# A start list and a written order for the filling and emptying of a software-pipelined two-layer graph transformer (fp32, one core)

## The chip, the cores and the metric

One core of a Trainium2 chip. The metric is the device time of one execution in microseconds; the median of three runs is shown. The engines are PE (matmul), ACT, DVE, POOL and SP, which here only issues DMAs. Each engine works through its own instruction list in order, and they meet by semaphores.

## The reference

For a batch of 128 graphs with 128 nodes and 256 channels, two layers follow one another.

```
layer A: q,k,v = x@W.T + b; 8 heads of 32; p = softmax(where(adj, q k^T, -16384))
         z = v; four times z = 0.9 * p @ z + 0.1 * v
         x = layernorm(x + z) * gamma + beta
layer B: n = ln1(x); q,k,v = n@w + b
         p = softmax(q k^T / sqrt(32) + (0.1*adj*adj where adj > 0, else -inf))
         x1 = x + (p @ v) @ wo + bo
         out = x1 + gelu(ln2(x1) @ w1 + b1) @ w2 + b2      # 256 -> 1024 -> 256
```

All is float32. The kernel keeps precision in large matmuls by splitting each operand into a rounded high part (fp32r) and a low part, the rest, and adds three products: high by high, high by low, low by high.

## The kernel before

Graphs are taken in pairs (`GB = 2`), 64 pairs `g`. The work of a pair is cut into 84 named steps, each a small function on each engine that takes part. Names: `lt`, `lx`, `laA`, `laB` load x turned (`xT`), x and the adjacency (SP); `xs` splits `xT` into `inT_A` (POOL, L657); `qA kA vA` project (PE L309 and L318, copied out by ACT and, for `vA`, DVE); `msA` masks (POOL); `sA` scores of all heads (PE L327); `mA00` to `mA11` add the mask and take maxima (DVE L534; digits: graph, half of the heads); `eA..` exps (ACT L437); `rA0`, `rA1` reciprocals (DVE); `wA0`, `wA1` normalise (POOL L678); `pA..` transpose the probabilities (PE L341, out by ACT for half 0, by DVE for half 1); `z0` to `z3` the hops (PE L357, out by ACT), each with `h0` to `h3`, which turns the result back (PE L367, out by DVE); `xv` prepares the residual (POOL). Layer norms are `y` (statistics, DVE), `i` (root, POOL), `n` (normalise, DVE), numbered 0 to 2; `g`, `b1`, `b2` add rows (POOL). `tB`, `tC` transpose a normalised input (PE L293; high part by ACT, low part by DVE). Layer B repeats `q k v s m e r w p` and then has `pv` (PE L376), `o` (L383), `u0` to `u3` (up, PE L391, gelu on ACT L463), `c0` to `c3` (low parts, DVE L612), `d0`, `d1` (down, PE L401), `st` (store).

What sets the order is one list, `ORDER`, with a lag beside each step: in turn i every engine goes through the list and does step `n` for pair `i - lag`. Lags go from 0 (`kA`, `qA`) to 5 (`tC`, `u`, `c`, `d`, `st`), so there are 64 + 5 = 69 turns, 0 to 68; in turns 0 to 4 and 64 to 68 steps whose pair does not exist are left out. `Timetable` (L85) builds the list. It also deals out the four PSUM banks of `ring_ps` in list order. Most buffers are single; `v_A`, `xv` and `probsT_A` are double.

Before the list there is a set-up (L229 to L233 on SP, L262 on PE, L478 on DVE). All 24 parameter tensors are loaded into space that the pairs use later (`probs`, `probsT_A`, `probsT_B`) with one semaphore, and PE, ACT, DVE and POOL wait for the whole of it:

```
WEIGHTS = 16 * (9 + 9 + 6)
pe.wait_ge(s_weights, WEIGHTS)      # so do ACT, DVE and POOL
```

PE then does the fold (52 small matmuls, L268 and L271: the shifts of the layer norms times the weights, to go into the biases), DVE adds it to the biases, scales the weights of layer B by the layer norms' gains, and writes all high parts, then all low parts. `s_ready` releases PE and ACT. POOL and SP begin the steps before that.

Of the kernel before, what the change touches and what calls it, by code (L numbers as in the profile page):

```python
# [96 lines left out]

def build(nc, x, xT, adj, WqT, bq, WkT, bk, WvT, bv, gamma, beta, ln1_g, ln1_b, ln2_g, ln2_b,
# [648 lines left out]
```

## Time and profile before

| | us |
|---|---|
| median of 3 runs | 2346.55 (2343.37 to 2348.0) |
| the profiled execution | 2345.26 |
| its span, first to last instruction | 2343.5 |
| granted TensorE clock, mean of the span | 0.995 |

The span is what the trace shows; 1.8 us of the profiled execution's own time lie around it. Times in rows are in microseconds from the span's start. Consecutive matmuls overlap, so a piece of PE work is best read from the start of one to the start of the next.

### The profile page before, as it was taken

Reading aid. Unit: us, or ns where it says so; the run is one execution under the profiler, and the core shown is the slowest. Engines: PE = TensorE matmul, PEld = TensorE weight load, DVE = VectorE, ACT = ScalarE, POOL = GpSimd, SP = SyncE. Lnnn points to the kernel's source line nnn. Section 1 sums busy time; section 2 is a strip of 40 time slices with the busy share of each in tenths; the row PEclk is TensorE's granted clock in tenths of the full one; section 3 lists DMA queues with packets and bytes.
Section 4 is the critical chain, followed back from the end, with each engine's and each line's share of the span. In section 5 each row is a group of like instructions: output and inputs, shape, how many; then the busy total and the mean of one; then the engine's idle time right before and its main releaser. Section 6 shows DMA issues by size and latency. Waiting matters only on the chain.

```text
span 2343.5 us, 77819 instructions
## 1 busy us (share of the span) xinstructions
PE 2262.8 (97%) x29492; PEld 2154.7 (92%) x29492; DVE 1729.5 (74%) x7009; ACT 1915.3 (82%) x6462; POOL 1515.4 (65%) x1610
## 2 busy tenths in 40 slices
PE   2799999999999999999999999999999999999987
PEld 2689999999999999999999999999999999999987
DVE  3478778778777777777777777877877877877863
ACT  0679889889889888888888888888988988988964
POOL 0676766666667666666666676676676666666652
PEclk9999999999999999999999999999999999999999
DMA  3110110110110110110111011011011011011000
GB/s 96 36 33 20 38 38 21 37 38 24 34 38 24 34 38 25 33 38 27 31 38 36 22 38 38 20 38 38 20 38 38 20 38 38 25 34 38 20 15 15
DMA packets 95729, 76.85 MB, mean 33 GB/s; under 512 B 9600, under 2 KB 95104, under 8 KB 95360
## 3 DMA queue, kind: packets, MB, share of 16 engines
q1 hardware_dynamic: 95360, 71.87, 10.0%
q8 instruction: 239, 3.92, 0.7%
q14 instruction: 130, 1.06, 0.1%
HBM read 55.06 MB, written 16.78 MB: 31 GB/s over the span
## 4 chain that ended last, share of the span: by engine, by line
PE 93%; ACT 3%; DVE 1%; issue 1%; POOL 0%; DMA 0%; ACTq 0%; DVEq 0%; POOLq 0%
PE ring_ps L290 41%; PE ring_ps L407 15%; PE ring_ps L353 13%; PE ring_ps L345 10%; PE score_ps L336 6%; PE ring_ps L373 5%; PE ring_ps L300 3%; ACT probs L441 1%; ACT hidden L469 0%; ACT hT_high L469 0%; POOL probs L683 0%; DVE w_low L506 0%; ACT zT L455 0%; DVE probs L541 0%; ACT L469 0%
## 5 line engine op out<-in xcount | busy, mean ns | idle before, releaser
L441 ACT ACTIVATE probs<-probs,negmax 128x128 f32<-128x128 f32 x2048 | 796.5, 397 | 11.7 <-DVE negmax L541 4.6
L683 POOL TENSOR_TENSOR probs<-probs,rinv 128x512 f32<-128x512 f32 x512 | 533.4, 1063 | 102.1 <-DVE rinv L555 101.9
L441 ACT ACTIVATION_READ_ACCUMULATOR probs<-probs,negmax 128x1 f32 x2048 | 399.8, 195 | 0.0
L455 ACT ACTIVATE zT<-ring_ps 128x512 f32<-128x512 f32 x256 | 158.4, 619 | 211.4 <-PE ring_ps L353 211.4
L290 PE MATMUL ring_ps<-inT_C_high,w_high 128*128 128x256 f32 x1024 | 301.7, 295 | 1.4 <-DVE inT_C_low L522 1.4
L345 PE MATMUL ring_ps<-ident,probs 128*128 128x128 f32 x2048 | 294.0, 276 | 6.6 <-POOL probs L683 4.8
L407 PE MATMUL ring_ps<-w_high,hT_high 128*128 128x256 f32 x1024 | 296.8, 290 | 2.0 <-ACT hT_high L469 1.5
L407 PE MATMUL ring_ps<-w_low,hT_high 128*128 128x256 f32 x1024 | 286.5, 280 | 0.0
L407 PE MATMUL ring_ps<-w_high,hT_low 128*128 128x256 f32 x1024 | 286.2, 279 | 0.0
L290 PE MATMUL ring_ps<-inT_C_high,w_low 128*128 128x256 f32 x1024 | 285.0, 278 | 0.0
L290 PE MATMUL ring_ps<-inT_C_low,w_high 128*128 128x256 f32 x1024 | 285.0, 278 | 0.0
L614 DVE TENSOR_TENSOR hT_low<-hidden,hT_high 128x512 fp32r<-128x512 f32 x256 | 223.2, 872 | 71.7 <-ACT hT_high L469 64.5
L345 PEld LDWEIGHTS ring_ps<-ident,probs 128*128 128x128 f32 x2048 | 227.7, 141 | 33.2 <-issue 27.2
L541 DVE CUSTOM_DVE_ANT_0 probs<-score_ps,mask_B 128x128 f32<-128x128 f32 x1024 | 228.5, 283 | 32.6 <-PE score_ps L336 32.6
L689 POOL TENSOR_TENSOR rstd<-moments,eps 128x2 f32<-128x2 f32 x192 | 37.8, 197 | 311.2 <-DVE moments L601 311.0
L541 DVE CUSTOM_DVE_ANT_0 probs<-score_ps,mask_A 128x128 f32<-128x128 f32 x1024 | 229.3, 283 | 7.8 <-issue 7.3
L469 ACT ACTIVATE hidden<-ring_ps,b_col 128x256 f32<-128x256 f32 x512 | 219.9, 494 | 5.0 <-PE ring_ps L290 4.2
L587 DVE TENSOR_TENSOR x<-ring_ps,x1b 128x512 f32<-128x512 f32 x64 | 44.3, 691 | 241.0 <-PE ring_ps L290 239.1
L469 ACT ACTIVATE hT_high<-ring_ps,b_col 128x256 fp32r<-128x256 f32 x512 | 222.0, 506 | 0.0
L353 PE MATMUL ring_ps<-probsT_A,z 128*32 128x128 f32 x6144 | 207.6, 276 | 7.5 <-DVE z L568 7.4
L290 PEld LDWEIGHTS ring_ps<-inT_C_high,w_high 128*128 128x128 f32 x1024 | 194.1, 190 | 2.4 <-DVE inT_C_low L522 2.0
L407 PEld LDWEIGHTS ring_ps<-w_high,hT_high 128*128 128x128 f32 x1024 | 192.4, 188 | 2.9 <-ACT hT_high L469 2.0
(148 smaller groups left out, 7362.7 us busy)
## 6 DMA issues: line engine op xcount, KB each, us to landing
xT_sb<-in_xT_dram SPq DMA_DIRECT2D x64, 256.0 KB, 3.2
x_sb<-in_x_dram SPq DMA_DIRECT2D x64, 256.0 KB, 2.9
out_dram<-x SPq DMA_DIRECT2D x128, 128.0 KB, 2.0
adj_A<-in_adj_dram SPq DMA_DIRECT2D x64, 128.0 KB, 3.1
adj_B<-in_adj_dram SPq DMA_DIRECT2D x64, 128.0 KB, 2.3
probsT_A<-in_L_gnn_w_dram SPq DMA_DIRECT2D x1, 1024.0 KB, 7.7
probsT_B<-in_L_gnn_w_dram SPq DMA_DIRECT2D x1, 1024.0 KB, 10.1
probs<-in_L_gnn_Wq_dram SPq DMA_DIRECT2D x1, 256.0 KB, 2.9
```

The lines of the kernel that those rows point to most:

```text
L290: mm = pe.matmul(dst, left(a, kc), right(b, kc), start=(n == 0), stop=(n == len(pairs) - 1))
L336: mm = pe.matmul(score_ps[:, r, (b * C + c) * P:(b * C + c + 1) * P], qT[l][r * HD:(r + 1) * HD, c, b * P:(b + 1) * P], kT[l][r * HD:(r + ...
L345: mm = pe.transpose(ring(name, g)[:, r * P:(r + 1) * P], probs[:, UNIT[l, b], half * HR + r, :], ident[:, :])
L353: mm = pe.matmul(ring(name, g)[r * HD:(r + 1) * HD, (b * C + c) * P:(b * C + c + 1) * P], src[:, b, h * HD:(h + 1) * HD], prT[:, b, h, :], ...
L373: mm = pe.transpose(ring(name, g)[:, at:at + P], zT[k][:, b, c, :], ident[:, :])
L407: mm = pe.matmul(ring(name, g)[:, 0:H], hT[a][:, f, b * P:(b + 1) * P], w2_p[c][:, f, :], start=(n == 0), stop=(n == len(pairs) - 1))
L441: e = act.activation(probs[:, u, h, :], probs[:, u, h, :], ACT.Exp, bias=negmax[:, u, h:h + 1], scale=-1.0, accum_out=sums[:, u, h:h + 1])
L455: act.activation(zT[k][:, :, :, :], ring(name, g).rearrange("p (b c n) -> p b c n", b=GB, c=C), ACT.Copy).then_inc(s_out[name], 1)
L469: e = act.activation(dst[:, i, :], ring(name, g)[:, i * T:(i + 1) * T], ACT.Gelu, bias=b1_col[:, 2 * f + i:2 * f + i + 1])
L541: t = dve.tensor_tensor_reduce(probs[:, u, h, :], score_ps[:, r, (b * C + half) * P:(b * C + half + 1) * P], mask[l][:, b, :], -1.0, HIGHE ...
L614: dve.tensor_tensor(hT[1][:, 2 * f:2 * f + 2, :], hidden[:, f % 2, :, :], hT[0][:, 2 * f:2 * f + 2, :], ALU.subtract).then_inc(s_h_low[nam ...
L683: pool.tensor_tensor(probs[:, u, hs, :], probs[:, u, hs, :], rinv[:, u, hs].unsqueeze(2).to_broadcast([P, HR, P]), ALU.mult).then_inc(s_pr ...
```

## The change

Three things, and what they need.

1. The start. Loads are issued in order of use, with ten semaphores instead of one; five small ones go out from ACT's queue. The first `xT`, adjacency and x are part of SP's start list. The three layer-A weights are split right away, each by its own ACT copy and DVE subtraction. All other set-up work becomes steps of the list, done once, in pair 0: `Wf` (the fold), `Wq Wk Wv`, `Wo`, `Wu0 Wu1`, `Wd0` to `Wd3` (high part on ACT with the gain as its scale; low part on DVE, for `Wd` on POOL). Raw weights lie in layer-B buffers only.
2. The first nine turns (0 to 8) and the last eight (61 to 68) are replaced by lists of their own, `HEAD` and `TAIL`, which hold the same steps of the same pairs in another order. In `TAIL` the number is the distance from the end: `.1` is the last pair.
3. Because the order differs there, steps in those lists and in turns 9 to 11 (`table.loose`) wait explicitly for the readers of the buffer that they overwrite; some semaphores are shared between steps and waited for by their count in the list (`table.nth`).

The PE steps in the two lists, in the order of the change:

```
HEAD: qA.0 kA.0 vA.0 sA.0 qA.1 kA.1 vA.1 sA.1 pA00.0 pA01.0 qA.2 pA10.0 pA11.0 kA.2 z0.0 h0.0 sA.2 z1.0 pA00.1 pA01.1 h1.0
 pA10.1 z2.0 pA11.1 h2.0 z0.1 z3.0 h0.1 h3.0 z1.1 vA.2 h1.1 Wf.0 z2.1 qA.3 h2.1 tB.0 z3.1 pA10.2 pA11.2 h3.1 kB.0 ...
TAIL: ... sB.4 z1.3 pv.5 d1.6 ... qB.3 kB.3 pA00.1 sB.3 tC.4 pA10.1 pA11.1 vA.1 pA01.1 vB.3 u0.4 z0.1 u1.4 pB00.3 pB01.3 u2.4
 h0.1 tB.2 u3.4 pB10.3 pB11.3 kB.2 qB.2 pv.3 z1.1 sB.2 d0.4 d1.4 h1.1 o.3 z2.1 h2.1 pB00.2 z3.1 pB01.2 h3.1 tC.3 vB.2
 pB10.2 u0.3 u1.3 pB11.2 u2.3 u3.3 pv.2 d0.3 tB.1 d1.3 qB.1 kB.1 o.2 sB.1 vB.1 tC.2 u0.2 u1.2 u2.2 u3.2 pB10.1 pB00.1
 pB11.1 pB01.1 d0.2 pv.1 d1.2 o.1 tC.1 u0.1 u1.1 u2.1 u3.1 d0.1 d1.1
```

The core of the diff:

```diff
+HEAD_TURNS = 9
+HEAD = """
+eb.0 qA.0 lx.0 laB.0 xs.0 laA.0 kA.0 eA00.0 vA.0 mA00.0 sA.0 msA.0 eA01.0 xs.1 mA01.0 lt.0 qA.1 lt.1 mA10.0 mA11.0
+kA.1 rA0.0 vA.1 mA00.1 sA.1 eA10.0 eA11.0 pA00.0 eA00.1 rA1.0 lt.2 pA01.0 qA.2 mA01.1 pA10.0 xv.0 msA.1 pA11.0 eA01.1
+wA0.0 rA0.1 xs.2 wA1.0 msB.0 Wd2.0 kA.2 z0.0 mA10.1 eA10.1 wA0.1 eA11.1 mA11.1 h0.0 sA.2 msA.2 wA1.1 z1.0 pA00.1 rA1.1
+Wd0.0 pA01.1 xv.1 h1.0 Wq.0 mA00.2 pA10.1 Wd3.0 z2.0 pA11.1 h2.0 Wv.0 Wu1.0 z0.1 z3.0 Wd1.0 i0.0 h0.1 xs.3 h3.0 y0.0
+g.0 Wk.0 z1.1 eA00.2 mA01.2 n0.0 mA10.2 vA.2 h1.1 eA01.2 msA.3 Wu0.0 mA11.2 y1.0 eA10.2 Wo.0 i1.0 Wf.0 eA11.2 rA1.2
...
+TAIL_TURNS = 8
...
-        self.steps = [(n, i - lag) for i in range(pairs + DEPTH) for n, lag in ENTRIES if 0 <= i - lag < pairs]
+        turns = [[(n, i - lag) for n, lag in ENTRIES if 0 <= i - lag < pairs] for i in range(pairs + DEPTH)]
+        head = [(n, int(g)) for n, g in (t.split(".") for t in HEAD.split())]
+        tail = [(n, pairs - int(g)) for n, g in (t.split(".") for t in TAIL.split())]
+        turns[:HEAD_TURNS] = [head]
+        turns[len(turns) - TAIL_TURNS:] = [tail]
+        self.steps = [s for turn in turns for s in turn]
+        self.loose = set(head + tail + [s for turn in turns[1:4] for s in turn])
...
         @block.sync
-            for t, w in loads: ...  for t, w in cols: ...  for t, w in rows: ...
+            weight(rawA["q"][:, :, :], WqT, "Aq")
+            sp.dma_start(xT_sb[:, :, :], xT_v[0]).then_inc(s_xT, 16)
+            weight(rawA["k"][:, :, :], WkT, "Ak")
+            weight(rawA["v"][:, :, :], WvT, "Av")
+            sp.dma_start(adj_sb["A"][:, :, :], adj_v[0]).then_inc(s_adj["A"], 16)
+            for n, w in (("q", wq), ("k", wk), ("v", wv)):
+                weight(rawB[n], w, "B")
+            weight(w1_raw, w1, "up")
+            column(h2_col, ln2_b, "up")
+            column(g2_col, ln2_g, "up")
+            sp.dma_start(x_sb[:, :, :], x_v[0]).then_inc(s_x, 16)
+            weight(rawB["o"], wo, "o")
+            for f, t in enumerate(w2_raw):
+                sp.dma_start(t[:, :, :], w2.rearrange("(c p) n -> p c n", p=P)[:, 2 * f:2 * f + 2, :]).then_inc(s_in["down"], 16)
+            for t, w in ((colB["q"], lbq), (colB["k"], lbk), (b1_col, b1)):
+                column(t, w, "rest")
+            for t, w in ((bvB_row, lbv), (gamma_row, gamma), (beta_row, beta), (bo_row, bo), (b2_row, b2)):
+                row(t, w, "rest")
...
         @block.tensor
-            pe.wait_ge(s_weights, WEIGHTS)
...
             def input_ready(g, l, n):
                 if l == "A":
                     pe.wait_ge(s_split, g + 1)
+                    if g == 0:
+                        pe.wait_ge(s_wA, "qkv".index(n) + 1)
...
         @block.scalar
+            for t, w, signal in ((colA["q"], bq, "colA"), (colA["k"], bk, "colA"), (h1_col, ln1_b, "B"), (g1_col, ln1_g, "B")):
+                act.dma_start(t[:, :], w.rearrange("(c p) -> p c", p=P), allow_slow_non_contiguous=True).then_inc(s_in[signal], 16)
+            act.dma_start(bvA_row[:, :], bv.partition_broadcast(P)).then_inc(s_in["bvA"], 16)
+            for n in "qkv":
+                act.wait_ge(s_in["A" + n], 16)
+                act.activation(wA[n][0][:, :, :], rawA[n][:, :, :], ACT.Copy).then_inc(s_whighA, 1)
+            def split_w(name, g, n):
+                act.wait_ge(s_in["B"], 16 * 5)
+                for kc in range(C):
+                    w = act.activation(wB[n][0][:, kc, :], rawB[n][:, kc, :], ACT.Copy, scale=g1_col[:, kc:kc + 1])
+                w.then_inc(s_whigh, 1)
...
         @block.vector
+            for done, n in enumerate("qkv"):
+                dve.wait_ge(s_whighA, done + 1)
+                dve.tensor_tensor(wA[n][1][:, :, :], rawA[n][:, :, :], wA[n][0][:, :, :], ALU.subtract).then_inc(s_wA, 1)
...
             def values(name, g, l):
-                if l == "A" and g:
-                    dve.wait_ge(s_xv, g)
+                if l == "A" and g >= 2:
+                    dve.wait_ge(s_xv, g - 1)
+                    dve.wait_ge(s_out["h2"], g - 1)
```

## Rows read from the trace of the kernel before

**Rows 1.** The page: busy time by engine, share of the span, instructions.
```profile
PE 2262.8 (97%) x29492; PEld 2154.7 (92%) x29492; DVE 1729.5 (74%) x7009; ACT 1915.3 (82%) x6462; POOL 1515.4 (65%) x1610
```

**Rows 2.** Chain of waits, whole span: start, length, what; the turn repeats.
```profile
203.95 2.83 PE ring_ps L290 x24
...
238.82 2.83 PE ring_ps L290 x24
...
2192.10 2.83 PE ring_ps L290 x24
```

**Rows 3.** Timeline of the start: start, length, engine, line, what [idle before].
```profile
0.72 0.44 SPq L229 DMA_DIRECT2D probs<-in_L_gnn_Wq_dram  x1
...
5.30 3.46 SPq L231 DMA_DIRECT2D colA_q<-in_L_gnn_bq_dram  x1
...
19.15 8.05 SPq L238 DMA_DIRECT2D xT_sb<-in_xT_dram  x2
24.07 0.48 DVE L482 TENSOR_SCALAR h_wide<-ones,h_col 128x128 f32<-128x128 f32 x2 [24.07 <-DMA b_row<-in_L_gnn_b_dram]
...
34.93 2.05 PE L271 MATMUL ring_ps<-probs,h_wide 128*128 128x256 f32 x4
...
54.28 0.58 PE L290 MATMUL ring_ps<-inT_A_high,wA_k_high 128*128 128x256 f32 x1 [17.30 <-DVE w_low L506]
```

**Rows 4.** DMA issues of 0 to 30 us: queue, size, median us to landing.
```profile
xT_sb<-in_xT_dram SPq DMA_DIRECT2D x2, 256.0 KB, 4.2
probs<-in_L_gnn_Wq_dram SPq DMA_DIRECT2D x1, 256.0 KB, 2.9
...
b_row<-in_L_gnn_b_dram SPq DMA_DIRECT2D x1, 128.0 KB, 5.4
```

**Rows 5.** Timeline again: first pieces of POOL, DVE and ACT, and matmuls.
```profile
24.84 0.61 POOL L662 CAST inT_A_high<-xT_sb 128x512 fp32r<-128x512 f32 x1 [23.14 <-DMA xT_sb<-in_xT_dram]
25.53 1.27 POOL L664 TENSOR_TENSOR inT_A_low<-xT_sb,inT_A_high 128x512 fp32r<-128x512 f32 x1
...
45.52 0.69 DVE L506 TENSOR_TENSOR wA_q_low<-probs,wA_q_high 128x512 fp32r<-128x512 f32 x1
...
57.32 1.28 ACT L433 ACT_TABLE_LOAD   x1 [57.32 <-PE ring_ps L290]
...
58.68 0.28 PE L290 MATMUL ring_ps<-inT_A_high,wA_q_low 128*128 128x256 f32 x1
```

**Rows 6.** Chain of waits, 54 to 146 us: start, length, what.
```profile
62.54 3.19 ACT probs L441 x16
...
74.03 1.05 PE ring_ps L353 x32
...
92.47 0.70 DVE y L574
...
101.94 0.88 PE ring_ps L300 x4
...
145.24 0.44 PE ring_ps L300 x4
```

**Rows 7.** Chain of waits, 2200 us to the end.
```profile
2203.16 0.44 PE ring_ps L300 x4
...
2231.66 1.10 PE score_ps L336 x32
...
2263.97 1.10 PE score_ps L336 x32
...
2294.23 1.15 PE score_ps L336 x32
...
2314.44 1.01 PE ring_ps L353 x32
```

**Rows 8.** Busy time by stretch (instructions), granted clock last but two.
```profile
1017.08:1051.96 34.88, 34.88 (x463) 33.32 (x461) 26.76 (x110) 29.95 (x103) 23.69 (x26) 1.00 0.10 33
...
54.28:101.94 47.66, 35.21 (x484) 30.63 (x485) 21.65 (x111) 27.51 (x104) 24.01 (x25) 0.96 0.09 26
```

More of the change, by code:

```diff
@@ new lines @@
+eA01.7 tB.5 eA10.7 pB11.4 mA11.7 eb.5 rA1.7 eA11.7 d1.3 h1.6 i0.5 qB.5 rA0.7 lt.8 kB.5 pv.4 mB00.5 z2.6 sB.5 pA00.7
+mB01.5 o.4 eB00.5 y2.4 wB1.4 pA10.7 h2.6 qA.8 g.5 mB10.5 kA.8 eB01.5 i1.5 n2.4 pA11.7 st.3 pA01.7 mB11.5 z3.6 msB.5
+laB.6 rB0.5
+"""
+TAIL_TURNS = 8
+TAIL = """
+laA.4 lt.3 h3.6 xs.4 wA0.5 tC.8 y0.6 eB10.7 z0.5 wA1.5 vA.4 eB11.7 eb.6 vB.7 h0.5 u0.8 sA.4 mA00.4 n0.6 z1.5 pB00.7
+xv.5 c0.8 u1.8 i2.8 lx.5 h1.5 msA.4 u2.8 u3.8 rB1.7 qA.3 z2.5 c1.8 c2.8 b1.7 mA01.4 pB10.7 xs.3 c3.8 y1.6 pB01.7
@@ L73 @@
     KINDS[f"d{_b}"] = ("down", _b)
+SET_UP = {"Wf": ("fold",), "Wo": ("split_o",)}
+for _n in "qkv":
+    SET_UP[f"W{_n}"] = ("split_w", _n)
+for _k in range(C):
+    SET_UP[f"Wu{_k}"] = ("split_up", _k)
+for _k in range(FC // 2):
+    SET_UP[f"Wd{_k}"] = ("split_down", _k)
 ENTRIES = [(t.split("/")[0], int(t.split("/")[1])) for t in ORDER.split()]
@@ L79 @@
 assert sorted(NAMES) == sorted(KINDS)
-RINGED = ("turn", "project", "values", "turn_probs", "hop", "turn_back", "attend", "output", "up", "down")
+KINDS.update(SET_UP)
+RINGED = ("fold", "turn", "project", "values", "turn_probs", "hop", "turn_back", "attend", "output", "up", "down")
+PER_LAYER = ("maxima", "exps", "recip")
+SHARED = {k: (k,) for k in PER_LAYER + ("low",)}
+SHARED.update({k: ("split",) for k in ("split_w", "split_o", "split_up", "split_down")})
 UNIT = {(l, b): 2 * "AB".index(l) + b for l in "AB" for b in range(GB)}
@@ L88, in __init__ @@
     def __init__(self, pairs):
-        self.steps = [(n, i - lag) for i in range(pairs + DEPTH) for n, lag in ENTRIES if 0 <= i - lag < pairs]
+        turns = [[(n, i - lag) for n, lag in ENTRIES if 0 <= i - lag < pairs] for i in range(pairs + DEPTH)]
[5 more added lines that the diff above has]
+        self.loose = set(head + tail + [s for turn in turns[1:4] for s in turn])
+        for n in NAMES:
+            assert [g for m, g in self.steps if m == n] == list(range(pairs))
+        self.nth, counted = {}, {}
+        for n, g in self.steps:
+            if KINDS[n][0] in SHARED and (KINDS[n][0] != "exps" or KINDS[n][3] == 1):
+                signal = SHARED[KINDS[n][0]] + KINDS[n][1:2] * (KINDS[n][0] in PER_LAYER)
+                counted[signal] = counted.get(signal, 0) + 1
+                self.nth[n, g] = counted[signal]
         ringed = [s for s in self.steps if KINDS[s[0]][0] in RINGED]
@@ L538, in maxima @@
                     dve.wait_ge(s_mask[l], g + 1)
+                if g and (name, g) in table.loose:
+                    dve.wait_ge(s_full[f"p{l}{b}{half}"], g)
                 for r in range(HR):
```

282 lines of the change are left out of this document (185 added, 97 removed).

## The prediction

> **What bounds the kernel now.** I read the page first. PE is busy 97% of the span, ACT 82%, DVE 74%, POOL 65% [rows 1]. So in the middle there is nothing to win; the question is how much of the span is not middle. The chain of waits over the whole span gives the period: its piece of two projections stands at 203.95, 238.82 and, 57 turns after the first, at 2192.10, so one turn is 34.88 us [rows 2]. The busy time of one such stretch shows why: PE 34.88 of 34.88, ACT 29.95, DVE 26.76, POOL 23.69 [rows 8]. A turn with all steps is one pair's worth of PE work, and 64 pairs are 64 x 34.88 = 2232.3 us. The span is 2343.5, so 111.2 us is lost to start, filling and emptying. Only this can change.
>
> To place it I price the PE steps by the same rows: 12 matmuls of 256 columns (a projection, `v`, `o`, an `up`) are 1.42, half of 2.83 [rows 2]; a `down` has 24, so 2.83; scores 1.10 and a transpose step 0.44 [rows 7]; a hop or `pv` 1.0 [rows 6]. They add to 34.7, within half a per cent of 34.88. Turns 0 to 4 hold, by their lags, 63.3 us of this work and turns 64 to 68 hold 111.1 (together five full turns). Turn 5 begins with its transposes at 145.24 [rows 6], turn 64 with the same step at 2203.16 [rows 7], 59 x 34.88 = 2057.9 later. So the head loses 145.2 - 63.3 = 81.9 and the tail 140.3 - 111.1 = 29.2.
>
> The head in three pieces. (a) The first matmul of a projection runs at 54.28 [rows 3]: all 24 parameter loads must land (the last at 24.07), then the fold runs on PE until 36.98, then DVE scales and splits every weight. Lost 54.3. (b) From there to the `tB` of pair 0 at 101.94 [rows 6] 47.7 us pass with 29.6 us of PE work in them: lost 18.1. (c) From there to 145.24, 43.3 us with 33.7 of work: lost 9.6.
>
> **The change part by part.**
>
> *The first matmul.* `WqT` is the first load on SP (0.72, landed 2.9 later, 3.6) [rows 3, 4]. ACT first issues five small loads, at about 0.5 each, until about 3.3, then pays a table load of 1.28 [rows 5] and a copy of 128x512 (the nearest DVE and POOL pieces of that size are 0.69 and 0.61 [rows 5]; I take 0.6): 5.5. DVE's low part, 0.69: 6.3. Beside it `xT` is issued at 1.2 and lands by 5.4 with the median of 4.2 [rows 4]; POOL's two instructions, 0.61 and 1.27 [rows 5]: 7.4. POOL is later, so `qA.0` starts at 7.4. Lowest, with a landing in 2.9: 6.1; highest, if one of ACT's issues stalls as `colA_q` did on SP (3.46 [rows 3]) and landings take 5.4 [rows 4]: 10. Piece (a) falls from 54.3 to 7.4, a gain of 46.9.
>
> Here the Trainium skill and a row differ. The trace has the table load at 1.28 and the copy behind it [rows 5]. The Trainium skill, "ScalarE: Activation LUTs", section "What ACT_TABLE_LOAD costs", puts a drain of about 1.4 us on top, some 2.66 in all. By it ACT's path would end at 7.7, beside POOL's 7.4, and the start would be 0.3 later; the sum stays with the row.
>
> *Pair 0 to its `tB`.* Before, from the first matmul to the first hop of pair 0 took 74.03 - 54.28 = 19.75 [rows 3, 6]. The new order puts `qA.1 kA.1 vA.1 sA.1` ahead of `pA00.0`, good filler, but it also puts `xs.1` ahead of `wA0.0` on POOL and `qA.1`, `kA.1` ahead of `eA10.0` on ACT. These need the second `xT`. Its DMA stands on SP behind the whole list of 25 start loads and `laB.0`. Before, 24 loads kept SP from 0.72 to 19.15 [rows 3], the columns stalling it; with four columns and one row gone to ACT and six bulk issues added I take 17.8 for its issue (13.8 if nothing stalls, 19.5 as before). Behind the rows it takes between 2.9 and 5.4 to land [rows 4]: about 22.5. Meanwhile pair 0 has done: `qA.0 kA.0` at the low clock, 4.7 (24 matmuls until 58.96 before, where 2.83 is the warm price [rows 2, 3, 5]), `vA`, `sA` until 14.5, the first exps at 15.8, half of them done at 18.9. Then ACT stands before `qA.1`. Split done 24.4; PE resumes slow after its idle, `kA.1` complete at 29.0, copied 29.9; the other 8 exps take 3.1 (16 records in 3.19 [rows 6]): 33.0; recip and POOL's two halves 2.3: 35.4; last transposes and `kA.2` in front: `z0.0` at 37.3, which is 29.9 after PE's start instead of 19.75. The delay of 10 is in no row of before; its bounds are 0 (second `xT` landed before 14.5) and 12.
>
> From `z0.0` to the end of `h3.0` took 18.4 before (74.03 to 92.47 [rows 6]). The new list puts `z` steps first and PE fills between with 0.4 to 2 us; I walk 13. In this chain ACT, DVE and POOL also do the weight splits. ACT: three layer-A copies earlier, then in the list six of 128x256, `wo`, two of 1024, four of 512: about 7.6. It is busy 27.5 of 47.7 there [rows 8], so most falls in its gaps; on the path I take 1.5, between 0 and 7.6. DVE has 21.7 and POOL 24.0 of 47.7 [rows 8]: their 5.6 and four subtractions of 1.27 are costed at nothing, ACT's copy before them being the later. Then the layer norms, 101.94 - 92.47 = 9.5 as before. `tB.0` stands at 37.3 + 13 + 1.5 + 9.5 = 61.3, before the fold is counted.
>
> *The fold* keeps its 52 matmuls, which took 24.7 to 36.98 = 12.3 at the low clock [rows 3]. 48 of them are bound by their weights, as the transposes are, which take 0.44 for four [rows 7]: 5.3, and 1.0 for the other four, so 6.3 warm. It is placed after `h1.1`, inside pair 0's layer-norm wait of 9.5 us, where the other steps of the list are 5.7. Together 12.0: `tB.0` is 2.5 late, 63.8. If hops are waiting there anyway it is 0; if PE is cold, 12.3 + 5.7 - 9.5 = 8.5.
>
> PE work before `tB.0` in the new list is 31.5 us without the fold, so at 63.8 the loss is 32.3 (7.4 of it the start, 24.9 piece (b), 6.8 more than before). Of piece (c), 9.6 before, I keep 4, between 0 and 9.6: layer-A steps of later pairs are further ahead as filler. Head: 36.3 instead of 81.9, a gain of 45.6.
>
> *The tail.* In before, `sB` of the last four pairs is followed by intervals of 34.9, 32.3 and 30.3 us (the first by the period) [rows 7]; the PE work in them is 34.9, 29.0 and 23.3. From the last `sB` (2294.23) to the last `pv` (2314.44) 20.2 pass with 13.2 of work, and from there 29.1 to the end with 17.0 [rows 7]. In the new list these two last stretches have the same PE steps; exps, gelus, two layer norms, stores follow one another, and their 19 lost us stay. In the three intervals the work is 42.1, 20.0 and 32.3: 7.2 more, layer-A work of the last pairs kept back, and `sB.2` stands before `d0.4 d1.4 o.3`, so exps begin under that work. If the idle of 3.3 + 7.0 were all filled the gain would be 10; chain-bound parts leave some. I take 6, between 0 and 10, and below nothing down to -4 if the delayed steps of pair 63 put `tB.1` late.
>
> *The middle* has the same list in turns 9 to 60; merged semaphores count the same events. Its extra waits sit on POOL and DVE, with 11 and 8 us of slack per turn [rows 8]. Cost 0.
>
> *Sum.* 2343.5 - 45.6 - 6 = 2291.9 span. The profiled execution took 2345.26, 1.8 more than its span: 2293.7. It lies 1.3 below the median of the runs shown, 2346.55, so a median of 2295.
>
> The Trainium skill, "DMA: Bandwidth & Descriptors", section "Issuing engines are not separate DMA queues", says that loads issued from a second engine save only the issuing sequencer's time. By it the five loads on ACT bring no landing forward and only shorten SP's list; the stall of 3.46 in `colA_q` [rows 3] is of the time it would save.
>
> **Rivals.**
> - *The second `xT` is no wait.* If SP runs through its list by 13.8 and the load lands before 17.5, `z0.0` comes about 8 earlier, and `eA10.0` is hardly held. For it: bulk issues are 0.44 each [rows 3]. Against: columns stalled SP. Time 2295 - 8 = 2287, and 2279 if the tail's idle and piece (c) fill as well.
> - *Less than the start is gained.* All 7.6 of ACT's split copies stand in pair 0's chain (+6) and later order gives nothing, tail and piece (c) losing what they lost (+6 and +5.6). For it: ACT is in order, and a copy placed between two hops holds the next `zT`. Against: such copies stand where its next result is not due. One of the two parts gives 2301 to 2307; I put it at 2304.
> - *The change doesn't do what it says:* loads wait for one another as before (the last row at 24) and PE starts at 25. 17.6 more: 2313. Against: the semaphores are per weight.
> - *Slower.* The order of turns 9 to 60 locks into another phase, where POOL or ACT ends late, and PE waits each turn. It decides from 51.6/52 = 0.99 us per turn, a turn of 35.87. ACT's slack of 4.9 per turn [rows 8] speaks against it. A lock 1.3 late gives 2295 + 68 = 2363.
>
> **How the numbers follow.** Forecast 0.47 (own range 2290 to 2300), early `xT` 0.25, less than the start 0.23, loads as before 0.03, slower 0.02. The range reaches from the early case with a good tail, 2279, to the top of the third, 2307. No change is what lies within 0.2%, 4.7 us; only a partial lock of 0.9 to 1.08 us per turn gives that, under 0.01. Faster 0.98, same 0.005, slower 0.015.
>
> **What would show it.** The first projection at 6 to 10 us. An idle PE of 8 to 11 us just before `qA.1`, its releaser POOL's split and behind it the DMA of `xT`; without it the first rival holds. First hop near 37, first `tB` near 64. The period 34.88 again; any other number there breaks the whole sum. From the last `pv` to the end 29 us. The forecast is wrong if the last full turns stand more than 58 or less than 38 us earlier than before.

## The result: 28 us faster, half of what was forecast

| kernel | median (lowest to highest), us | runs | profiled execution, its span |
|---|---|---|---|
| before | 2344.96 (2342.82 to 2348.0) | 4 | 2345.26, 2343.5 |
| after | 2317.08 (2315.57 to 2317.8) | 4 | 2317.23, 2315.4 |

The ratio is 0.9881, 95% interval 0.9869 to 0.9893: faster, by 27.9 us. The forecast was 2295 with a range of 2279 to 2307, so the time lies 10 us above the range.

The page of after, busy time by engine, stands against [rows 1]: the same matmuls (29492) and nearly the same work on the others, in a shorter span.

```profile
PE 2266.6 (98%) x29492; PEld 2154.3 (93%) x29492; DVE 1749.9 (76%) x6993; ACT 1926.8 (83%) x6478; POOL 1520.4 (66%) x1613
```

The middle is what it was. Busy time by stretch (sum, then PE, PEld, DVE, ACT, POOL with instructions, granted clock last but two) for one turn of after, against the first line of [rows 8]; and the timeline's transposes of one step 29 turns apart, (2032.98 - 1021.46) / 29 = 34.88:

```profile
1021.46:1056.34 34.88, 34.88 (x463) 33.32 (x461) 26.76 (x110) 29.95 (x103) 23.64 (x26) 1.00 0.11 32
```
```profile
1021.46 0.60 PE L402 MATMUL ring_ps<-ident,n 128*128 128x128 f32 x4
...
2032.98 0.60 PE L402 MATMUL ring_ps<-ident,n 128*128 128x128 f32 x4
```

So all of the difference is at the two ends. As mark I take the transposes `tC` of pair 4, with which turn 9 begins: 284.60 before, 254.04 after. The head gained 30.6. From that mark to the end of the span it is 2058.9 before and 2061.4 after. The tail lost 2.5.

The timeline of after's start (start, length, engine, line, what; in brackets the idle time before it and what ended it), against [rows 3, 5]:

```profile
3.33 1.28 ACT L530 ACT_TABLE_LOAD   x1 [3.33 <-issue]
4.62 0.63 ACT L530 ACTIVATE wA_q_high<-qT_B 128x512 fp32r<-128x512 f32 x1
...
5.94 1.58 POOL L843 TENSOR_TENSOR inT_A_low<-xT_sb,inT_A_high 128x512 fp32r<-128x512 f32 x1
...
7.62 0.55 PE L377 MATMUL ring_ps<-inT_A_high,wA_q_high 128*128 128x256 f32 x1 [7.62 <-POOL inT_A_low L843]
...
19.58 0.43 SPq L344 DMA_DIRECT2D adj_B<-in_adj_dram  x1
20.05 8.11 SPq L338 DMA_DIRECT2D xT_sb<-in_xT_dram  x2
25.07 0.42 DVE L670 SCALAR_TENSOR_TENSOR edges<-adj_B 128x256 f32<-128x256 int32 x1 [15.69 <-DMA adj_B<-in_adj_dram]
...
25.81 0.61 POOL L841 CAST inT_A_high<-xT_sb 128x512 fp32r<-128x512 f32 x1 [15.38 <-DMA xT_sb<-in_xT_dram]
...
26.97 0.40 ACT L580 ACTIVATE probs<-probs,negmax 128x128 f32<-128x128 f32 x1 [13.01 <-DVE negmax L704]
...
27.83 0.58 PE L377 MATMUL ring_ps<-inT_A_high,wA_q_high 128*128 128x256 f32 x1 [11.97 <-POOL inT_A_low L843]
```

The start came as forecast: the first projection at 7.62 instead of 54.28. The activation stands directly behind the table load (3.33 + 1.28 = 4.61, then 4.62). The drain of about 1.4 us that the Trainium skill, "ScalarE: Activation LUTs", section "What ACT_TABLE_LOAD costs", puts beside it isn't seen here, nor in the middle (a load of 1.28 at 1027.08, the activation behind it at 1028.38).

Then two waits run side by side. PE idles 11.97 until POOL has split the second `xT`, which SP issues at 20.05, behind its whole list; that was in the forecast, 3 us earlier. The other was not. The very first step of the list, `eb.0`, is DVE's edge mask of layer B. It needs `adj_B`, which SP issues at 19.58. DVE stands before it until 25.07, and with it `vA.0`, the row maxima, and ACT's exps of pair 0, which begin at 26.97 (idle 13.01, released by DVE's `negmax`) where I had 15.8.

The same view from the first hop to the first `tB`, PE only, against [rows 6]:

```profile
42.15 1.08 PE L459 MATMUL ring_ps<-probsT_A,v_A 128*32 128x128 f32 x32
...
61.79 1.84 PE L388 MATMUL ring_ps<-h_col,probs 128*128 128x1 f32 x16
63.49 5.86 PE L388 MATMUL ring_ps<-h_col,probsT_B 128*128 128x1 f32 x32
69.22 2.05 PE L391 MATMUL ring_ps<-probs,h_col 128*128 128x256 f32 x4
71.20 1.94 PE L459 MATMUL ring_ps<-probsT_A,z 128*32 128x128 f32 x32
...
75.86 0.60 PE L402 MATMUL ring_ps<-ident,nx 128*128 128x128 f32 x4
```

The fold is the three middle pieces, 61.79 to 71.2: 9.4 us. Its first 16 one-column matmuls take 1.7, the next 32 take 5.7. The stretches of that time show why:

```profile
61.80:66.00 4.20, 4.20 (x35) 4.20 (x34) 4.20 (x17) 4.20 (x18) 3.75 (x4) 0.85 0.01 4
66.00:71.00 5.00, 5.00 (x20) 4.37 (x20) 4.04 (x14) 2.54 (x11) 2.66 (x4) 0.50 0.02 5
71.00:76.00 5.00, 5.00 (x51) 4.33 (x51) 2.22 (x8) 0.97 (x2) 3.60 (x4) 0.60 0.46 128
```

PE is busy 5.00 of 5.00 from 66 to 71, until 69.2 with matmuls of one column and then with the four of 256, and the granted clock there is 0.50, the 1.2 GHz level; behind the fold it is 0.60 until 76. In before the 48 one-column matmuls took 10.2 (24.70 to 34.93), 0.21 each. There the profile lists the clock as 1.00, so the low clock is read from their spacing.

Beside the fold, DVE and POOL in the same stretch: pair 0's layer norm begins with its `y` at 58.69 and ends with `tB` at 75.86, 17.2 instead of the 9.5 of before [rows 6]. POOL has `x` ready at 66.63, but DVE takes its statistics at 68.47, since it is in a low part of a weight and has four maxima behind it:

```profile
58.69 0.68 DVE L744 SCALAR_TENSOR_TENSOR y<-ring_ps,xv 128x512 f32<-128x512 f32 x1
...
65.35 1.28 POOL L883 TENSOR_TENSOR x<-x,beta_row 128x512 f32<-128x512 f32 x1
...
65.81 1.90 DVE L663 SCALAR_TENSOR_TENSOR w_low<-probsT_B,g_col,w_high 128x1024 fp32r<-128x1024 f32 x1
...
68.47 0.74 DVE L769 BATCH_NORM_STATS2 stats<-x 128x6 f32<-128x256 f32 x2
```

The stretch is also longer for another reason, which the timelines of DVE and POOL show. DVE scales `y`, and later `nx`, in two halves. In before the pair of halves takes 0.74 while POOL is idle (first line); in the kernel with the new lists but the old set-up (e7 below) it takes 2.06 and POOL works beside it nearly the whole time (the other three):

```profile
95.34 0.74 DVE L608 TENSOR_SCALAR y<-y,moments,rstd 128x256 f32<-128x256 f32 x2 [0.20 <-POOL rstd L692]
```
```profile
92.67 0.61 POOL L786 CAST inT_A_high<-xT_sb 128x512 fp32r<-128x512 f32 x1
92.72 2.06 DVE L731 TENSOR_SCALAR y<-y,moments,rstd 128x256 f32<-128x256 f32 x2 [0.29 <-POOL rstd L816]
...
93.36 1.26 POOL L788 TENSOR_TENSOR inT_A_low<-xT_sb,inT_A_high 128x512 fp32r<-128x512 f32 x1
```

At the other end, the timeline's scores and `pv` of the last pairs, against [rows 7]:

```profile
2204.10 1.17 PE L442 MATMUL score_ps<-kT_B,qT_B 32*128 32x128 f32 x32 [0.54 <-issue]
...
2227.59 1.17 PE L442 MATMUL score_ps<-kT_B,qT_B 32*128 32x128 f32 x32
...
2263.85 1.17 PE L442 MATMUL score_ps<-kT_B,qT_B 32*128 32x128 f32 x32
...
2285.61 1.08 PE L459 MATMUL ring_ps<-probsT_B,v_B 128*32 128x128 f32 x32
```

The intervals from the `sB` of the fourth last pair (2161.01) on are 43.1, 23.5 and 36.3 with 42.1, 20.0 and 32.3 of PE work in them: 8.5 lost, where it was 10.3 before and 4.3 in the forecast. Then the last two stretches, which I had left as they were:

```profile
2263.85:2285.70 21.85, 15.91 (x141) 14.87 (x144) 12.76 (x51) 16.16 (x53) 7.47 (x8) 0.84 0.00 1
2285.70:2315.40 29.70, 20.77 (x168) 19.56 (x168) 8.27 (x17) 7.32 (x18) 2.16 (x3) 0.83 0.06 19
```

They take 21.8 and 29.7 instead of 20.2 and 29.1 [rows 7], with the same PE steps; the granted clock is 0.84 and 0.83, before it was 0.92 and 0.88. The timeline of after at the start of the first of them shows what is late:

```profile
2269.34 0.78 PE L402 MATMUL ring_ps<-ident,n 128*128 128x128 f32 x4 [2.71 <-DVE n L784]
...
2270.04 0.69 DVE L692 TENSOR_TENSOR v_B<-ring_ps,bvB_row 128x512 f32<-128x512 f32 x1
2270.64 1.23 DVE L714 SCALAR_TENSOR_TENSOR scaled<-negmax,sums 128x8 f32<-128x8 f32 x1
...
2272.03 0.64 DVE L675 TENSOR_TENSOR inT_C_low<-ring_ps,inT_C_high 128x512 fp32r<-128x512 f32 x1
...
2272.72 0.58 PE L377 MATMUL ring_ps<-inT_C_high,w_high 128*128 128x256 f32 x1 [2.60 <-DVE inT_C_low L675]
```

Between the transposes of pair 62 and the low part that the `up` matmuls need, DVE now has `v_B` and a `scaled` of the last pair. In before it had a `scaled` there too, but that took 0.17 with POOL idle (2300.72), and here it takes 1.23 beside POOL's addition of `bo` (2270.59 to 2271.85). The low part is done 8.8 after the scores (2272.67 - 2263.85), in before's trace 7.5 (2301.68 - 2294.16), and PE idles 2.60 in front of it. That is 1.3 of the 1.6.

### The profile page after: what moved, and what is told of

Its sections match the earlier page's. It is cut to its first block and busy times, and to the rows that moved or that the text cites. A ratio compares the mean times of both kernels' runs of the same rounds, so it can differ in the third digit from the quotient of the medians.

```text
span 2315.4 us, 78263 instructions
## 1 busy us (share of the span) xinstructions
PE 2266.6 (98%) x29492; PEld 2154.3 (93%) x29492; DVE 1749.9 (76%) x6993; ACT 1926.8 (83%) x6478; POOL 1520.4 (66%) x1613
## 5 line engine op out<-in xcount | busy, mean ns | idle before, releaser
L790 DVE TENSOR_TENSOR hT_low<-hidden,hT_high 128x512 fp32r<-128x512 f32 x256 | 231.4, 905 | 62.5 <-ACT hT_high L621 56.2
L377 PEld LDWEIGHTS ring_ps<-inT_C_low,w_high 128*128 128x128 f32 x1024 | 195.2, 191 | 0.0
```

The lines of the kernel that those rows point to most:

```text
L377: mm = pe.matmul(dst, left(a, kc), right(b, kc), start=(n == 0), stop=(n == len(pairs) - 1))
L790: dve.tensor_tensor(hT[1][:, 2 * f:2 * f + 2, :], hidden[:, f % 2, :, :], hT[0][:, 2 * f:2 * f + 2, :], ALU.subtract).then_inc(s_h_low, 1)
```

## The experiments

All were timed beside the kernel before. A median carries about 0.15% of uncertainty, 3.3 us, so single steps are read from the marks of one profiled execution each: the first exp of pair 0 and its first hop; from the hop to `y`, with which its layer norm begins; from there to the first `tB`; from there to turn 9; and from turn 9 to the end of the span. All in us.

| kernel | median | ratio, 95% | first exp | first hop | hop to `y` | `y` to `tB` | `tB` to turn 9 | turn 9 | to the end |
|---|---|---|---|---|---|---|---|---|---|
| before | 2344.96 | 1 | 62.54 | 74.03 | 18.4 | 9.5 | 182.7 | 284.60 | 2058.9 |
| after | 2317.08 | 0.9881 (0.9869-0.9893) | 26.97 | 42.15 | 16.5 | 17.2 | 178.2 | 254.04 | 2061.4 |
| e1 | 2315.67 | 0.9876 (0.9861-0.9890) | 17.04 | 40.48 | 15.6 | 17.2 | 178.4 | 251.62 | 2061.7 |
| e2 | 2315.61 | 0.9874 (0.9859-0.9888) | 28.08 | 41.35 | 15.2 | 17.0 | 178.9 | 252.48 | 2061.3 |
| e3 | 2311.47 | 0.9858 (0.9844-0.9873) | 16.58 | 38.38 | 15.7 | 17.2 | 178.6 | 249.89 | 2061.4 |
| e4 | 2312.87 | 0.9865 (0.9848-0.9881) | 26.96 | 40.57 | 15.3 | 14.5 | 177.9 | 248.20 | 2061.8 |
| e5 | 2314.16 | 0.9867 (0.9852-0.9883) | 27.48 | 41.99 | 16.7 | 17.0 | 178.4 | 254.07 | 2060.3 |
| e6 | 2322.90 | 0.9902 (0.9888-0.9917) | 17.38 | 36.44 | 27.0 | 15.8 | 180.4 | 259.56 | 2060.6 |
| e7 | 2344.09 | 0.9993 (0.9984-1.0002) | 64.15 | 76.67 | 13.2 | 12.4 | 177.7 | 279.97 | 2062.3 |
| e8 | 2315.68 | 0.9874 (0.9857-0.9890) | 26.49 | 40.37 | 15.2 | 14.6 | 177.5 | 247.68 | 2062.6 |
| e9 | 2306.45 | 0.9837 (0.9822-0.9852) | 16.01 | 30.72 | 15.6 | 17.2 | 178.2 | 241.65 | 2061.7 |
| e10 | 2311.06 | 0.9859 (0.9843-0.9876) | 15.84 | 40.47 | 16.0 | 14.5 | 177.7 | 248.64 | 2060.8 |
| e11 | 2311.73 | 0.9860 (0.9845-0.9874) | 16.10 | 39.79 | 15.8 | 14.5 | 180.3 | 250.43 | 2059.8 |
| e12 | 2302.59 | 0.9819 (0.9803-0.9836) | 16.84 | 29.58 | 15.9 | 14.6 | 179.5 | 239.52 | 2061.5 |

How well these repeat: e5 has after's head and agrees within 0.3 from the first hop on; e11 has e10's head and differs by 1.8 at turn 9; e8 differs from after in the fold alone and yet is 1.8 ahead at the hop, long before it. In after the matmuls of `qA.1`, begun at 27.83 at 0.21 us apart, go over to 0.12 apart at 33.97, in e8 they begin at 27.32 and do so at 30.88, in e5 28.31 and 32.97. So a difference of under 2 us in hop or turn 9 proves nothing. The stretch from `y` to `tB` repeats within 0.2.

**e1: the edge mask later on DVE.**

```diff
-eb.0 qA.0 lx.0 laB.0 ...
+qA.0 lx.0 laB.0 ...
-wA0.0 rA0.1 xs.2 wA1.0 msB.0 ...
+wA0.0 rA0.1 xs.2 wA1.0 eb.0 msB.0 ...
```

> The changed kernel with one step moved: eb.0 (DVE, waits for the adjacency of layer B) stands just before msB.0 instead of first. Theory 1 (the head is short because pair 0's chain is late: DVE stood behind eb.0 until 25.1 us, and the second xT landed at 25.8): alone it gives almost nothing, since the last 8 exps of pair 0 wait for the copy of kA.1, which waits for the second xT: first exp near 17 instead of 27, first hop still at 41 to 42, time 2315 to 2317. Theory 2 (the first exps are the stall that counts): first hop 8 to 10 us earlier, 2307 to 2310.

As the first theory said: the first exp moved 10 us forward, the first hop only 1.7 and turn 9 2.4, hardly more than chance. The second exps of pair 0 and the last transposes still stand behind `qA.1` and its `xT`; timeline of e1, where PE's idle is as long as before:

```profile
17.04 0.40 ACT L580 ACTIVATE probs<-probs,negmax 128x128 f32<-128x128 f32 x1 [2.78 <-DVE negmax L704]
```
```profile
27.61 0.58 PE L377 MATMUL ring_ps<-inT_A_high,wA_q_high 128*128 128x256 f32 x1 [11.61 <-POOL inT_A_low L843]
```

**e2: the second `xT` right behind x in SP's list.**

```diff
             sp.dma_start(x_sb[:, :, :], x_v[0]).then_inc(s_x, 16)
+            sp.wait_ge(s_split, 1)
+            sp.dma_start(xT_sb[:, :, :], xT_v[1]).then_inc(s_xT, 16)
...
-                if g:
+                if g >= 2:
```

> The changed kernel with the second xT load taken from behind the start list to the place behind the load of x (about 8 us; it waits for the first split). Theory 1: qA.1 starts near 17 to 18 instead of 27.8, but the exps still wait for eb.0 until 27; the 16 exps then run without the break of 4 us, first hop near 38 instead of 42.2, time 2312 to 2315. Theory 3 (the head is bound later, in turns 3 to 8, by throughput of ACT and DVE): first hop earlier, time unchanged, 2316 to 2318.

`qA.1` starts at 17.53, as expected, but the hop stands at 41.35 and not near 38, a miss. Turn 9 moved 1.6. Alone, this too frees nothing: the first exp waits for the edge mask until 28.08, and the last exp of pair 0 ends at 35.7.

**e3: both.**

> Both edits together: eb.0 late and second xT early. Theory 1: first exp near 17, first hop near 27 to 29 instead of 42.2, first tB near 62 instead of 75.9, turn 9 starts 8 to 13 us earlier, time 2304 to 2309; more than the sum of the two alone. Theory 3: the first hop moves, turn 9 and the time don't, 2314 to 2318.

The hop moved 3.8, turn 9 4.2 and the time 5.6. I had expected a hop before 30. The timeline of POOL, with PE's gap, names the next wait of the same kind: the mask of pair 1 needs an adjacency tile issued at 21.39, and `wA0.0` of pair 0 stands behind it on POOL.

```profile
18.11 0.39 PE L379 MATMUL ring_ps<-inT_A_high,wA_q_high 128*128 128x256 f32 x1 [2.57 <-POOL inT_A_low L845]
```
```profile
27.83 1.07 POOL L830 TENSOR_SCALAR mask_A<-adj_A 128x256 f32<-128x256 int32 x1 [7.42 <-DMA adj_A<-in_adj_dram]
```

**e9: every load of the first two pairs early.** e1 and e2, and in SP's list also the second `adj_A` and the first `adj_B` behind `xT`, and the third `xT` ahead of the five rows.

```diff
             sp.dma_start(x_sb[:, :, :], x_v[0]).then_inc(s_x, 16)
+            sp.wait_ge(s_split, 1)
+            sp.dma_start(xT_sb[:, :, :], xT_v[1]).then_inc(s_xT, 16)
             weight(rawB["o"], wo, "o")
+            sp.wait_ge(s_mask["A"], 1)
+            sp.dma_start(adj_sb["A"][:, :, :], adj_v[1]).then_inc(s_adj["A"], 16)
+            sp.dma_start(adj_sb["B"][:, :, :], adj_v[0]).then_inc(s_adj["B"], 16)
...
+            sp.wait_ge(s_split, 2)
+            sp.dma_start(xT_sb[:, :, :], xT_v[2]).then_inc(s_xT, 16)
...
```

> The changed kernel with eb.0 late and all four loads that pair 0 came to wait for ahead in SP's list: second xT, second adjacency of layer A, first of layer B, and the third xT ahead of the five rows. Theory 1 (with only two of them early, e3 still waited 7.4 us on POOL for the second adjacency and then for the third xT, first hop 38.4): first hop at 29 to 32, first tB at 61 to 65, time 2302 to 2308. Theory 3 (what is gained before the first tB is lost again before turn 9, as ACT and DVE are then near full): first tB moves as said, turn 9 not, 2309 to 2313.

As expected by the first theory: 2306.45, its interval clear of after's, and turn 9 at 241.65, 12.4 earlier. The first hop is at 30.72, 11.4 earlier. It is the fastest of the kernels with the whole computation, 37.6 us below the kernel before beside which it ran (2344.07). PE's idle before `qA.1` shrank from 11.97 to 2.65:

```profile
17.63 0.38 PE L383 MATMUL ring_ps<-inT_A_high,wA_q_high 128*128 128x256 f32 x1 [2.65 <-POOL inT_A_low L849]
...
30.72 1.08 PE L465 MATMUL ring_ps<-probsT_A,v_A 128*32 128x128 f32 x32
```

**e4: the fold in PE's gap, ahead of `qA.1`.**

```diff
-... eA01.0 xs.1 mA01.0 lt.0 qA.1 lt.1 mA10.0 mA11.0
+... eA01.0 xs.1 mA01.0 mA10.0 mA11.0 Wf.0 lt.0 qA.1 lt.1
-g.0 Wk.0 ... y1.0 eA10.2 Wo.0 i1.0 Wf.0 eA11.2 rA1.2
+g.0 Wk.0 ... y1.0 eA10.2 Wo.0 i1.0 eA11.2 rA1.2
```

> The changed kernel with the fold Wf.0 (and mA10.0, mA11.0) put ahead of qA.1, into PE's idle 12 us of 16 to 28, the other loads as they are. Theory 1 (the fold's 9.4 us at 61.8 to 71.2 held tB.0): fold at 16 to 28.5 at the low clock, first tB near 69 instead of 75.9, time 2309 to 2313. Rival (tB.0 was held by the layer norms, the fold lay beside them): time 2316 to 2318.

The fold ran from 15.98 to 24.2, in the gap that was there anyway. `y` to `tB` is 14.5 instead of 17.2: at its old place the fold had cost 2.7. Turn 9 moved 5.8, of which the other half, before `y`, is within what repeats badly.

**e8: 46 of the fold's 48 one-column matmuls are left out**, with what they would add to the biases.

```diff
-                for n, (w, h, m) in enumerate([(rawB["q"], h1_col, c) for c in range(C)] + ...
+                for n, (w, h, m) in enumerate([(rawB["q"], h1_col, 0)]):
```

> The changed kernel with 46 of the 48 one-column matmuls of the fold left out (the folded biases are then not those of the reference). Theory 1 (the fold holds the first tB by its 9.4 us on PE, and leaves PE at the low clock for the 4 us behind it): first tB at 67.5 to 70, time 2308 to 2312. Rival (the fold lies in a wait anyway): tB at 74 to 76, time 2315 to 2318.

`y` to `tB` is 14.6, so the price of the fold there is 2.6, as e4 says; of the 6.4 at turn 9 the rest stands mostly before `y`, where the fold isn't. The marks and the median disagree on the two theories: `tB` at 70.19 is nearly the first one's, the time of 2315.68 is the rival's. The median moved 1.4, its runs spread from 2312.1 to 2317.0, and the profiled one is the lowest.

**e12: e9 with e8's small fold.**

> e9 (four loads early) with 46 of the 48 one-column matmuls of the fold left out (folded biases not the reference's): the price of the fold where the loads no longer hold pair 0. Theory 1 (loads and fold are separate terms and add): first tB 5 to 8 us earlier than e9's 63.5, turn 9 near 235 to 237 instead of 241.7, time 2299 to 2302; turn 9 is then earlier than the 239 that the forecast stands for. Rival (with the loads early the fold lies in a wait, or its gain is lost before turn 9): turn 9 at 239.5 or later, time 2304 to 2307.

`tB` came 3.4 earlier than in e9, not 5 to 8, and turn 9 at 239.52 is where the rival put it; the time of 2302.59 lies between the two theories. Again `y` to `tB` is 2.6 shorter; 1.3 of it is given back by turn 9. What holds `tB` without the fold is in this stretch of e12: DVE is busy 10.89 of 11.00, PE 5.88.

```profile
49.00:60.00 11.00, 5.88 (x53) 4.53 (x52) 10.89 (x35) 7.49 (x29) 8.20 (x10) 0.73 0.18 55
```

**e10: e9 with the fold on PE behind `sA.1`, its part on DVE behind `pA01.0`; e11: that with the old tail.**

```diff
-kA.1 rA0.0 vA.1 mA00.1 sA.1 eA10.0 ...
+kA.1 rA0.0 vA.1 mA00.1 sA.1 Wf.0 eA10.0 ...
-g.0 Wk.0 ... y1.0 eA10.2 Wo.0 i1.0 Wf.0 eA11.2 rA1.2
+g.0 Wk.0 ... y1.0 eA10.2 Wo.0 i1.0 eA11.2 rA1.2
...
-                        "spread": spread, "norm": norm, "low": low, "down": down})
+                        "spread": spread, "norm": norm, "low": low, "down": down}, ("pA01", 0))
```

> e9 with the fold's matmuls put behind sA.1, where PE waits for pair 0's exps, and DVE's part of it behind its copy of pA01.0. Theory 1: first tB 5 to 8 us earlier than in e9 (55 to 59), time 2297 to 2303. Theory 3: no more than 2 us less than e9.

A miss: 4.6 slower than e9. With the loads early, the place that was a gap in e4 is one no more. The fold took 24.65 to 34.0, ahead of `pA00.0` in PE's queue, and DVE stood before the next maxima for 10.71. First hop 40.47 instead of 30.72, for 2.7 won behind `y`. Stretches of e10, again with the clock at 0.50 in the fold, and DVE's wait:

```profile
24.60:28.00 3.40, 3.40 (x36) 3.35 (x30) 0.00 (x0) 1.61 (x9) 1.15 (x1) 0.99 0.43 129
28.00:34.00 6.00, 6.00 (x25) 5.53 (x25) 0.00 (x0) 0.00 (x0) 0.00 (x0) 0.50 0.19 63
```
```profile
35.06 0.29 DVE L713 CUSTOM_DVE_ANT_0 probs<-score_ps,mask_A 128x128 f32<-128x128 f32 x1 [10.71 <-PE ring_ps L460]
```

**e5: after with `TAIL` in the old order** (in e11, e10 with the same edit).

> The changed kernel with TAIL put back into the order of before (turns 61 to 68 from the list of lags); start and head as changed. Theory 1 (the new tail lost 2.5 us where 6 were forecast as gain, since turn 61 starts 30.6 us earlier than before and the end comes only 28.1 earlier): the end comes 2 to 3 us earlier, 2313 to 2315.5. Rival (the new tail order is a gain and something else at the end took it): 2320 to 2324.

> e10 with the last eight turns in the order of before. Theory 1: 2 to 3 us less than e10, 2295 to 2300; the forecast's own place for the change was 2295. Rival (the new tail is worth keeping): 3 us or more above e10.

The medians don't decide: 2.9 lower in e5, 0.7 higher in e11, all inside the intervals. The last column says a little more. Two pairs of kernels differ in the tail alone: e5 needs 1.1 less than after from turn 9 to the end, e11 1.0 less than e10. That is small beside the spread of this column: with the new tail order eleven kernels, whatever their head, need 2060.6 to 2062.6 (mean 2061.6), with the old order three need 2058.9 (before), 2060.3 and 2059.8 (mean 2059.7). Before and e7, which differ in the head too, are 3.4 apart. The two groups don't overlap, by 0.3. So no kernel shows a gain by the new tail order, and it costs 1 to 2 us. The expectation for e11, 2295 to 2300, missed by 12, most of it the miss of e10, on which it built.

**e6: after with `HEAD` in the old order**, the weight steps inserted.

> The changed start (loads one by one, splits as steps) under the old order of the first nine turns, with the W steps put into turn 2 and the fold ahead of the first tB. Theory 1 (the new head order lost time, because it lets pair 0 wait behind loads of layer B and of pair 1 that stand behind the start list): pair 0's chain runs as before from a start at 7.7 us, first hop near 28 to 31, first tB at 57 to 62, turn 9 at 243 to 248 instead of 254, time 2305 to 2311. Rival (the new head order gains by its filler what the loads cost): turn 9 at 255 to 260, time 2318 to 2323.

2322.9, turn 9 at 259.56: 5.5 later than after, past the range of the first theory and in that of the rival. The first hop is the earlier one, but from there to `y` 27.0 pass. In the timeline pair 0's transposes on PE wait for POOL, which until 25.74 stood 15.19 for the second `xT` (`xs.1` is ahead of `wA0.0` in the old order too), and later transposes between its hops wait once more:

```profile
28.75 2.11 PE L451 MATMUL ring_ps<-ident,probs 128*128 128x128 f32 x8 [10.79 <-POOL probs L862]
...
53.35 1.12 PE L451 MATMUL ring_ps<-ident,probs 128*128 128x128 f32 x4 [3.66 <-POOL probs L862]
```

**e7: the other half: before's set-up with the new `HEAD` and `TAIL`** (without the weight steps).

> The other half alone: the set-up of before (all loads, fold and splits ahead of the first step) with the new orders HEAD and TAIL, without their W steps. With all loads landed before the first step, the order shows its own worth. Theory 1 (the order is good when loads are early: forecast 9 us in the head at best; tail loses 2.5): first tB 43 to 47 us after PE's start at 54.3, turn 9 at 276 to 281 instead of 284.6, time 2338 to 2343. Rival (order worth nothing or less): 2345 to 2350.

2344.09, ratio 0.9993 with 1 inside the interval; the time lies between the two theories. Turn 9 is in the first one's range, the first `tB` at 102.25, 48 us behind 54.3, isn't. The head gains 4.6 at turn 9, the tail gives 3.4 of it back. The two halves agree: the new order of the head is worth 4.6 alone and 5.5 with the new start, the new start 25.0 (284.60 to 259.56). And e7 has the new lists without splits and fold: hop to `y` 13.2, `y` to `tB` 12.4.

## Why the prediction was wrong

Right were the large term and the middle. Piece (a) ended at 7.62 (forecast 7.4), the turn is 34.88, and PE idles before `qA.1` for the second `xT`, 11.97 for 8 to 11. The test that I had named failed: the last full turns stand 30.6 earlier, not 38 to 58. The span was forecast at 2291.9 and came at 2315.4. The 23.5 us between are five terms, each by the marks of the table.

| step of the forecast | forecast | measured | miss |
|---|---|---|---|
| first hop | 37.3 | 42.15 | 4.9 |
| hop to `y` (walk 13, splits 1.5) | 14.5 | 16.5 | 2.0 |
| `y` to `tB` (norms 9.5, fold 2.5) | 12.0 | 17.2 | 5.2 |
| piece (c) | 4 | 6.9 | 2.9 |
| tail | -6 | +2.5 | 8.5 |

**The first hop.** The failed step is "the first exps at 15.8, half of them done at 18.9": they began at 26.97. I had followed the new list on PE, POOL and ACT, but not on DVE, whose first entry waits for the last load but one. And the second `xT` was issued at 20.05, not 17.8. The two waits lie side by side, and a third behind them, the second adjacency on POOL, I didn't see (e3: 7.42 idle); that is why e1 and e2 alone show next to nothing and e9 moves the hop by 11.4. The delay against the 19.75 of before from PE's start to the hop, which I put at 10 with an upper bound of 12, is 14.8 in after and about 3 in e9.

**Hop to `y`.** The walk was right: e7, with the new list and no splits, needs 13.2. With the splits it is 15.2 to 16.7, so they cost at least 2.0 there, not 1.5. What is above that goes in part with the clock: in after and e5, at 16.5 and 16.7, the granted clock is 0.90 over this stretch, in the others, at 15.2 to 16.0, it is 1.00. One of the splits' pieces on DVE, the two halves of `wB_q_low` at 49.44, takes 2.75 beside POOL, where `wB_k_low` of the same size takes 0.85 at 60.36.

**`y` to `tB`.** The failed step is "Then the layer norms, 101.94 - 92.47 = 9.5 as before". The new list alone makes them 12.4 (e7), with the splits they are 14.5 (e4, e8), with the fold 17.2. Of the 2.9 of the list 2.6 are two instructions of DVE: the scalings of `y` and `nx` take 2.06 and 2.17 beside POOL's work in e7, where they took 0.74 with POOL idle and 0.91 beside POOL in before. This is not one bad place: all 15 such pairs of after between 61 and 226 take 1.29 to 2.17, in the middle they take 0.73 or 0.92, and in e6, with the old order, pair 0's take 0.74 each. The order of before leaves POOL idle, or in one instruction of its own, when DVE scales; the new one doesn't. No run moves POOL's work by itself, so this is read from the traces and not tested.

The 2.1 of the splits is the difference of e7 and e8. DVE's low parts in this stretch of after add up to 3.4 (0.85, 1.90 and 0.66; the 1.90 is beside POOL, its twin at 55.15 takes 1.27), but e7 also lacks ACT's copies, and the two aren't separated. They were costed at nothing because DVE had slack, 21.7 busy of 47.7 [rows 8]. In the stretch they fell in it had little; the busy time of before from `y` to `tB` (us, then PE, PEld, DVE, ACT, POOL) shows DVE at 8.16 of 9.47:

```profile
92.47:101.94 9.47, 5.92 (x116) 4.86 (x117) 8.16 (x34) 4.12 (x19) 5.31 (x7) 1.00 0.01 2
```

The fold itself, 2.6 to 2.7 at this place, was priced right at 2.5, though by luck: its matmuls took 9.4 and not the 6.3 of a warm PE, and the wait they were set into was 14.5 and not 9.5.

**Piece (c).** Lost until turn 9 were 51.2 us (254.04 less 202.8 of PE work), 44.4 of them until `tB` (75.86 less 31.5). Keeping 4 of the 9.6 was the term that was too small. The new list makes the way from `tB` to turn 9 177.5 to 180.3 long in all twelve kernels that have it, 177.7 in e7, which has neither splits nor fold. That is 6.4 more than the 171.3 of work, so nearly all of the 6.9 is there without the set-up's work. The slow scalings above lie in this stretch too; whether they are what holds it no run shows, and the cause stays open.

**The tail.** "I take 6, between 0 and 10" failed: the tail lost 2.5. Only the outer bound of -4 holds, and the late step that the trace shows is the low part for the `up` matmuls of pair 62, not the `tB.1` that was named for it. The idle in the three intervals fell by only 1.8, from 10.3 to 8.5. The last two stretches, called unchanged, grew by 2.2: PE's steps in them are the same, the order on DVE and POOL is not. The remaining 2.1 are ahead of the fourth last `sB`, or in my count of the work. Put back alone, the old order gives 1.1 and 1.0 (e5, e11), so the gain of 6 isn't there and the rest of the 2.5 is within the 2.0 by which kernels with one tail differ. Why the filler brought no more than 1.8 wasn't tested.

By its number the rival "the change doesn't do what it says", for 2313, came nearest, but its mechanism is refuted: PE starts at 7.62, not at 25. By mechanism "less than the start is gained", for 2304, did. It had tail and piece (c) right in kind; of the 7.6 us of ACT's copies that it put in the chain, at most 2 to 3.5 us are there before `y` (the splits' cost by e7, DVE's part included), and another 2.1 behind it. The first rival, an early `xT`, describes e9 rather than after. What the Trainium skill, "DMA: Bandwidth & Descriptors", section "Issuing engines are not separate DMA queues", says of loads issued by ACT no run here tests by itself.

Still open: what holds piece (c), the rest of the tail, a fold or low parts cut into smaller pieces, an order that keeps POOL clear of DVE's scalings, and e9 with the old tail, which by e5 and e11 would be some 1 us below e9. None of these was tried.

## What to carry to other kernels

- An order written by hand for a start has to be read once for every in-order queue, the one that issues the loads included, from its first entry. A step that waits for a late load holds all behind it, and such waits lie side by side: removing one showed 1.6 and 2.4 us at turn 9 here, all of them 12.
- Slack of an engine over a long stretch is no price for what is placed in a chain: here DVE was busy 21.7 of 47.7 us, but 8.16 of the 9.47 us from `y` to `tB`, where the new pieces fell. Read the share of the very stretch. And the same piece of work that was free in PE's gap (e4) put the first hop 10 us back where the gap had gone (e10).
- An instruction's length in the old order is no constant in a new one. Look at what the neighbour engine does beside it: with POOL at work beside them DVE's scalings went from 0.74 to 2.06.
- Filler for a tail is judged on all engines: if PE's order stays and that of DVE and POOL changes, the stretch has changed.
